# Sending the last two images' output products half by half, and seven unread products at the start in place of five

## The reference

```python
x = x + _L0_conv_ref(_gn(x), ...)   # channel attention, 8 heads, output product with a bias
x = x + _L1_conv_ref(_gn(x), ...)   # below
# _L1_conv_ref
t = jnp.einsum('bchw,oc->bohw', x, w_in)
tf = jnp.fft.rfft2(tp, axes=(3, 5)); tf = tf * fft_filter[None, :, None, :, None, :]   # on 8 x 8 patches
t = jax.lax.conv_general_dilated(t, w_dw, window_strides=(1, 1), padding='SAME', feature_group_count=hid, ...)
x1, x2 = (t[:, :hid // 2], t[:, hid // 2:])
g = jax.nn.gelu(x1, approximate=False) * x2
return jnp.einsum('bchw,oc->bohw', g, w_out)
```

## Time and profile before

| | us |
|---|---|
| median of 3 runs | 68.55 (68.52, 68.55, 69.21) |
| the profiled execution, device time | 68.19 |
| the profiled execution, span from first to last instruction | 66.4 |
| PE busy in that span | 59.0 (89%) |
| VectorE busy | 40.9 (62%) |
| ScalarE busy | 34.5 (52%) |
| GpSimd busy | 22.2 (33%) |

### The profile page before, as it was taken

One profiled execution on the slowest core, in us unless ns is written; L12 is line 12 of the kernel. 1 busy time (PEld: TensorE's weight loads), 2 busy tenths in 40 slices (PEclk: granted clock), 3 DMA queues, 4 the chain that ended last, 5 costly groups with the idle time before them and its releaser, 6 DMA issues.

```text
span 66.4 us, 1346 instructions
## 1 busy us (share of the span) xinstructions
PE 59.0 (89%) x428; PEld 48.4 (73%) x428; DVE 40.9 (62%) x158; ACT 34.5 (52%) x88; POOL 22.2 (33%) x39
## 2 busy tenths in 40 slices
PE   3939999999999999999999999999999999979200
PEld 3929999979796989989899999889759651403000
DVE  0000035696416979699999859899998698870000
ACT  0710300037089466953519998968598614442920
POOL 3031003915160314330301599829397540000000
PEclk9999999999999999999999999999999999999999
DMA  0899999996000000000000000000000701520392
GB/s 0 239 340 268 368 239 260 247 262 197 25 0 0 5 0 0 0 0 10 0 0 5 0 0 0 10 0 0 15 5 20 236 11 35 149 93 0 83 307 84
DMA packets 3427, 5.83 MB, mean 88 GB/s; under 512 B 642, under 2 KB 1820, under 8 KB 3420
## 3 DMA queue, kind: packets, MB, share of 16 engines
q1 hardware_dynamic: 3004, 5.45, 28.8%
q10 hardware_dynamic: 416, 0.29, 1.9%
HBM read 4.04 MB, written 1.57 MB: 85 GB/s over the span
## 4 chain that ended last, share of the span: by engine, by line
PE 69%; DVE 7%; DMA 5%; ACT 4%; issue 3%; ACTq 1%; DVEq 1%; POOLq 1%; POOL 1%; SPq 1%
PE CH L735 26%; PE CV L735 18%; PE AB L735 15%; PE VB L735 10%; DMA XT<-in_xT 5%; DVE AB L723 3%; ACT X L538 2%; DVE AB L704 2%; DVE GT L729 2%; ACTq L272 1%; POOL CD L493 1%; POOLq L272 1%; DVEq L272 1%; ACT GE L578 1%; SPq L414 1%
## 5 line engine op out<-in xcount | busy, mean ns | idle before, releaser
L735 PE MATMUL AB<-CST,XT 128*97 128x128 f32 x64 | 9.4, 294 | 1.0 <-DMA XT<-in_xT 1.0
L486 POOL TENSOR_TENSOR ZP<-ZP,TURNED 128x512 f32<-128x512 f32 x6 | 7.6, 1271 | 5.9 <-ACT TURNED L533 5.8
L735 PEld LDWEIGHTS AB<-CST,XT 128*97 128x97 f32 x64 | 8.1, 178 | 1.3 <-DMA XT<-in_xT 1.3
L514 ACT ACTIVATE XF<-AB 97x512 f32<-97x512 f32 x8 | 4.7, 587 | 3.9 <-PE AB L735 3.9
L735 PEld LDWEIGHTS CH<-CST,ZA 128*128 128x128 f32 x48 | 5.8, 192 | 0.9 <-issue 0.8
L735 PE MATMUL CH<-CST,ZA 128*128 128x80 f32 x48 | 6.3, 275 | 0.0
L538 ACT ACTIVATE X<-CV,ST 96x512 f32<-96x512 f32 x6 | 3.8, 678 | 4.7 <-PE CV L735 4.7
L735 PE MATMUL CV<-X,AT 96*96 96x512 f32 x12 | 6.0, 597 | 0.0
L597 DVE COPY GI<-CH 97x97 f32<-97x97 f32 x2 | 0.5, 252 | 8.1 <-PE CH L735 8.1
L532 ACT ACTIVATE TURNED<-ZQ 64x512 f32<-64x512 f32 x6 | 3.8, 628 | 2.0 <-DVE ZQ L688 1.9
L475 POOL TENSOR_TENSOR RN<-NRM,POWER 96x2 f32<-96x2 f32 x4 | 2.8, 690 | 5.9 <-DVE NRM L639 5.9
(11 more groups left out here) (154 smaller groups left out, 130.2 us busy)
## 6 DMA issues: line engine op xcount, KB each, us to landing
X<-in_x SPq DMA_DIRECT2D x4, 384.0 KB, 8.3
out<-X SPq DMA_DIRECT2D x8, 192.0 KB, 2.2
XT<-in_xT SPq DMA_DIRECT2D x3, 388.0 KB, 6.3
XT<-in_xT SPq DMA_DIRECT2D x2, 194.0 KB, 3.2
WTS<-in_weights SPq DMA_DIRECT2D x1, 168.0 KB, 7.4
X<-GT SPq DMA_DIRECT2D x4, 32.0 KB, 1.9
WTS<-in_weights ACTq DMA_DIRECT2D x1, 126.9 KB, 5.4
LATE<-in_late SPq DMA_DIRECT2D x1, 109.5 KB, 6.8
```

The source lines that it names most:

```text
L486: ins = nc.gpsimd.tensor_tensor(ZP[:, b - 1, of], ZP[:, b - 1, of], TURNED[:, b - 1, of], ALU.add)
L514: nc.scalar.activation(XF[:, b, HALF * h:HALF * (h + 1)], bank[0:C1, :], ACT.Copy).then_inc(a_free, 1)
L735: return nc.tensor.matmul(o, lhsT, rhs, start=start, stop=stop)
```

## The change

The last entries of `PE_ORDER`, `final.3 final.0`, become `final.3.0 final.3.1 final.0.0 final.0.1`. A `final` step with a half waits only for that half's gate, and issues only that half's product; a `final` step without one (images 1 and 2) does what it did. The list `PROJECTED` and ScalarE's wait count in halves now. The number of unread products at the start goes from 5 to 7.

```diff
-    base.3.0 base.3.1 base.0.1 final.3 final.0
+    base.3.0 base.3.1 base.0.1 final.3.0 final.3.1 final.0.0 final.0.1
...
-PROJECTED = [s for s in PE_ORDER if s[0] == "final"]
+PROJECTED = [("final", s[1], h) for s in PE_ORDER if s[0] == "final" for h in s[2:] or range(2)]
...
-FILLERS = 5
+FILLERS = 7
...
-                    act.wait_ge(f_full, 2 * PROJECTED.index(("final", b)) + h + 1)
+                    act.wait_ge(f_full, through(PROJECTED, step))
...
-                    pe.wait_ge(gate_set, max(through(GATE_STEPS, ("gate", of, 0)), through(GATE_STEPS, ("gate", of, 1))))
-                    if step == PROJECTED[0]:
+                    halves = step[2:] or range(2)
+                    pe.wait_ge(gate_set, max(through(GATE_STEPS, ("gate", of, h)) for h in halves))
+                    if ("final", b, halves[0]) == PROJECTED[0]:
                         pe.wait_ge(out_in, 16)
-                    for h in range(2):
+                    for h in halves:
```

## The result

| | before | changed |
|---|---|---|
| median, all executions | 68.78 us (22, 68.03 to 71.03) | 68.72 us (22, 67.20 to 79.25) |
| ratio of the compared executions | | 0.9883 [0.9835, 0.9931] |
| the profiled execution, time / span | 68.19 / 66.4 | 69.54 / 67.7 |

The ratio compares only executions within 1.5% of the fastest of their own kernel, which are more than half of the 22 before and 5 of the 22 of the changed kernel; the plain medians contain all. On the first median of 68.55 the ratio gives 67.75. That is a gain of 1.2% between the lower ends of the two spreads, and there is next to none in the medians, so the 1.2% is not what an execution gains on average.

A forecast was written before the change was run, and what follows sets the result against it. PE held 69% of the chain, but gates and ScalarE's copies bound the end and GpSimd's powers shift.0. From 68.19 us, -0.57 at the end and -0.08 to 0 at the beginning gave 67.6, range 67.3 to 68.2.

The forecast's parts named there:

- The end: Last output products: half 0 no longer waits for gate 1, one ScalarE copy moves into idle time, 0.57 us earlier.
- the rival of lost pairing: Last output products: halves no longer stream side by side once a wait separates them; 68.0 to 68.7 us, chance 0.08.
- the landing of the last transfer: Last output DMA after ScalarE's copies: landing stays at up to 2.5 us or shrinks to 2.2; gain taken as 0.
- The start, direct cost: Two more products on FILL, 0.86 us of PE time, end at 4.41 inside PE's idle time; cost nothing.
- The start, the clock: TensorE's clock rises between 4.6 and 8.7 us; PE up to 2.0 us sooner, of which some 0.08 remain.
- the cover: At shift.0: GpSimd's powers, behind a copy waiting for the weights' DMA, hold SHIFT to 13.30 at best, hiding PE's gain.
- the reading of the spread: Start of the kernel: slower executions explained by a clock rise later than 8.7 us, inferred from four times.
- the 0.36 us: Start: the median's distance from the profiled execution, given back by an earlier, unbroken start of TensorE's clock.
- the rival that was given 0.04: PE's idle time before shift.0 takes the clock to 1.2 GHz, costing 2.05 us: 69.7 us, chance 0.04.
- The prediction's own sign of being wrong: The middle, 14 to 58 us, moving by more than 0.2 us, which nothing but the clock would explain.
- The evidence held against it: End of the profile: granted clock stays 1.00 to 66.3 although PE did 0.04 us of work after 61.8.

The follow-up runs named there:

- e2_fill7: The kernel before with 7 unread products at the start in place of 5, output products as before; 69.73 us median, ratio 0.988.
- e5_pool7: The changed kernel with GpSimd's copy into WVU, which waits for the late weights, moved behind the powers of all four images; 66.32 us median, ratio 0.973.
- e6_pool5: The changed kernel with the same move of GpSimd's WVU copy as e5_pool7, but 5 unread products; 67.43 us median, ratio 0.987.
- e3_moved: The changed kernel with PE's steps spec.2.1 and spec.1.0 moved forward, ahead of shift.0 and project.0; 68.55 us median.

## Why the prediction was right, and where it wasn't

**The end: right.** One copy of ScalarE moved into idle time. The forecast was 0.57 us to the start of the last copy; every pair of traces gives 0.56 to 0.58. PE starts image 3's half 0 at 61.13, 0.14 behind its gate instead of 0.05, and ScalarE reads it 1.13 later, as taken. The halves need not start as a pair to overlap, so the rival of lost pairing is out: in the changed kernel half 1's passes, from 61.76, run beside the others, and all eight are through 2.59 us after the first began (63.72 - 61.13). One after another, at the 0.43 us between the two passes of a lone product, they would take about 3.6 (7 x 0.43 + 0.59, an estimate). One term was mis-sized, the landing of the last transfer, which was taken to stay or shrink. From the last copy to the end of the span it takes 2.91 to 3.00 us in the four traces with both halves at once, and 2.97 to 3.11, on average 0.1 more, in the nine with the halves apart. Why is not shown. The end is worth about 0.45 to 0.5.

**The start, direct cost: right.** 14 passes end at 4.41, and cost nothing in the profiled execution.

**The start, the clock: right in kind.** It rose much earlier, and PE came to stand at shift.0 behind GpSimd and the late weights, as the cover was named: 1.35 us in the changed kernel, 1.48 in `e2_fill7`. No trace shows a gain at shift.0 itself: it starts at 13.86 and 13.63 there, and at 13.59 in the kernel before. `e5_pool7` against `e6_pool5` shows what the cover hid, 1.1 us by the medians and 0.8 by the traces.

**What failed was the reading of the spread**: "The median would be explained by a rise at about 9.4, the slowest by one at about 10.7". The four traces with 5 unread products show rises at 8.7, 9.0, 8.1 and 8.6 us (from the change of the 128x97 passes' pace), and PE's list ahead of shift.0 ends at 13.4 to 13.7 in all of them. What varies more is when the late weights land: the copy starts between 10.75 and 12.26, and in the traces that still wait for it shift.0 follows at 13.52 to 14.81. So no trace supports the 0.36 us that the forecast gave back through the clock, and the late weights explain a spread of that size without it. A late rise in an execution without a trace isn't excluded. The mean granted clock can't tell, since that column reads 1.00 before the rise too.

The nearness of 67.6 to 67.75 is in part luck. The end gives its 0.5; the rest of the 0.8 is a comparison of the fastest 5 of 22 executions of one kernel with the faster half of the other's. Over the 14 executions without a drop the gain is 0.33, over all of them 0.06.

**And the rival that was given 0.04 is half of the result**: that the idle time before shift.0 takes the clock down. The mean clock says that it happened in 8 of 22 executions, not in all, which is why the medians show next to no gain. The prediction's own sign of being wrong came up with it: the middle was to stay within 0.2 us but for the clock, and it moved by 1.6. The evidence held against it, a granted clock of 1.00 for 4.5 us behind the last product, was of the kind that misleads: in the changed kernel the column falls to 0.50 from 66.7, 2.9 us behind the end of the last product (63.72), where in the kernel before it had not fallen 4.5 us behind it. When it falls varies from execution to execution, and one without a fall proves little. The price in the profiled execution was 1.6 us instead of 2.05.

The Trainium skill, page "TensorE: Matmul & The Clock Gate", Part 1, section "HAM oscillation", describes idle gaps between bursts that take the clock back to half pace and make each burst start slow. The gaps of its example are DMA waits of about 3 to 5 us. The traces agree that idle time does it, but with shorter waits: 1.14, 1.35, 1.48 and 2.50 us ahead of four drops. The fifth, behind two waits of 0.5, does not fit that description.

## What to carry to other kernels

Before making one engine faster, find the next thing late at the same place, and who waits there when it is early: here a clock that rose 2 to 3.4 us sooner gained nothing at shift.0 until a copy that nobody needed yet was moved from ahead of four powers, and then about 1 us. Idle time of TensorE isn't free even off the critical path, since it can lower the clock for the work behind it; remove its cause, as `e5_pool7` did, or try to fill it. Taking dense passes away from between tiny ones came with long drops in 2 of 6 and 4 of 12 executions. When executions of one kernel spread by more than the effect, compare stretches between two fixed events in the traces: 3.59 against 3.02 us repeated to 0.01 while the times scattered by 2 us.

## What the runs showed of the hardware

- Two products in different partitions of the array overlap also when they start 0.6 us apart, and a later product's pass can start before an earlier product's second one: CH<-GT at 62.06, CV<-GT at 62.27, in the rows above. The Trainium skill, page "TensorE: Matmul & The Clock Gate", Part 3, section "What overlaps and what doesn't", says that matmuls start and end strictly in program order; this trace disagrees for the passes of float32 products.
- The granted-clock column is 1.00 in the first microseconds whatever the passes say (368 ns against 248). Behind the first rise it and the passes agree: the 128x128 passes take 403 ns on average (one of them still at the faster pace in part) right behind the drop at 15.5 us, as this row of the changed kernel, 15.7 to 16.1 us, shows:

```profile
L735 PE MATMUL AB<-CST,XT 128*97 128x128 f32 x3 | 0.8, 403 | 0.0
```

- A drop cost a little under half of its length here: 3.4 us at half pace cost 1.6, and the 13.6 us in `e3_moved` cost 6.0 (52.2 us from shift.0 to the last gate's end against 46.2).
